# Query and key low parts moved forward, strided reciprocals, and one look-ahead low part ahead of the gated product, in an attention and FFN layer

## The reference

```
qu, ku, vu, qc, kc, vc = split(xn @ W_qkv.T)          # each 8 heads x 512 x 64
term1     = where(causal, 0, (qc*s) @ vu.T)
lookahead = where(causal, sigmoid((qu*s) @ ku.T), 0)
Su        = term1 @ lookahead.T
scores    = where(causal, -max, (qc*s) @ kc.T - silu(Su))
out       = softmax(scores) @ vc ; out @ W_out.T
```

## Time and profile before

| | |
|---|---|
| median of 3 runs | 1061.36 us (1061.29 to 1063.61) |
| profiled execution, own time | 1063.24 us |
| its span | 1061.3 us |
| TensorE busy | 1038.1 us, 98% |
| VectorE busy | 888.6 us, 84% |
| ScalarE busy | 753.2 us, 71% |
| GpSimd busy | 565.1 us, 53% |
| granted TensorE clock | full speed throughout |

### The profile page before, as it was taken

One profiled execution on the slowest core, in us unless ns is written; L12 is line 12 of the kernel. 1 busy time (PEld: TensorE's weight loads), 2 busy tenths in 40 slices (PEclk: granted clock), 3 DMA queues, 4 the chain that ended last, 5 costly groups with the idle time before them and its releaser, 6 DMA issues.

```text
span 1061.3 us, 21352 instructions
## 1 busy us (share of the span) xinstructions
PE 1038.1 (98%) x7472; PEld 926.5 (87%) x7472; DVE 888.6 (84%) x1831; ACT 753.2 (71%) x1453; POOL 565.1 (53%) x630
## 2 busy tenths in 40 slices
PE   6999999999999999999999999999999989999997
PEld 5888888888888888888888888888888878899987
DVE  5798899889988998899889988998888878767665
ACT  6678777877787778777877787778777765443433
POOL 5365565556555655565556555656555546322230
PEclk9999999999999999999999999999999999999999
DMA  5054555565555555555555555654545965566632
GB/s 198 1 110 95 137 133 120 130 146 124 116 134 135 135 110 140 123 147 110 140 113 156 110 140 103 161 110 110 122 99 114 244 197 198 168 200 221 206 121 61
DMA packets 362716, 144.30 MB, mean 136 GB/s; under 512 B 254832, under 2 KB 343664, under 8 KB 360560
## 3 DMA queue, kind: packets, MB, share of 16 engines
q1 hardware_dynamic: 362608, 142.91, 53.2%
HBM read 76.55 MB, written 66.32 MB: 135 GB/s over the span
## 4 chain that ended last, share of the span: by engine, by line
PE 64%; ACT 16%; DVE 11%; POOL 4%; issue 4%; DMA 0%; ACTq 0%; POOLq 0%; DVEq 0%
PE X L850 17%; PE X L765 13%; PE X L1001 8%; PE X L992 6%; ACT prob L1191 5%; PE X L902 4%; PE X L834 4%; PE X L818 4%; PE X L804 4%; POOL prob L685 4%; ACT L_s L1175 3%; ACT T_s L1169 3%; PE X L789 3%; DVE gate L1485 2%; ACT PT_s L1221 2%
## 5 line engine op out<-in xcount | busy, mean ns | idle before, releaser
L685 POOL TENSOR_SCALAR prob<-prob,inv 128x512 f32<-128x512 f32 (+3 forms) x256 | 304.0, 1203 | 20.4 <-DVE inv L1515 20.4
L850 PE MATMUL X<-L_s,T_s 128*128 128x128 f32 (+3 forms) x1920 | 275.9, 301 | 2.5 <-DVE L_s L1471 2.2
L850 PEld LDWEIGHTS X<-L_s,T_s 128*128 128x128 f32 x1920 | 265.4, 189 | 13.9 <-issue 3.3
L765 PE MATMUL X<-xT,W 128*128 128x512 f32 (+1 forms) x972 | 244.5, 398 | 0.0
L765 PEld LDWEIGHTS X<-xT,W 128*128 128x128 f32 x972 | 175.6, 191 | 40.7 <-issue 0.4
L1183 ACT ACTIVATE gate<-X 128x1024 f32<-128x1024 f32 (+1 forms) x96 | 84.8, 884 | 157.2 <-PE X L850 157.1
L675 POOL TENSOR_SCALAR_AFFINE_SELECT T_s<-T_s 128x512 fp32r<-128x512 f32 x128 | 106.2, 842 | 102.1 <-DVE T_s L1478 102.1
L1191 ACT ACTIVATE prob<-prob,least 128x512 f32<-128x512 f32 (+3 forms) x256 | 141.8, 587 | 1.5 <-DVE least L1503 1.5
L1478 DVE TENSOR_TENSOR T_s<-X,T_s 128x1024 fp32r<-128x1024 f32 (+1 forms) x96 | 100.5, 1047 | 43.9 <-ACT T_s L1169 43.3
L659 POOL TENSOR_SCALAR_AFFINE_SELECT gate<-gate 128x256 f32<-128x256 f32 (+1 forms) x96 | 47.2, 495 | 163.1 <-DVE gate L1485 163.1
L1503 DVE CUSTOM_DVE_ANT_0 prob<-X,gate 128x512 f32<-128x512 f32 (+3 forms) x256 | 112.5, 486 | 8.0 <-issue 6.8
(11 more groups left out here) (111 smaller groups left out, 1876.0 us busy)
## 6 DMA issues: line engine op xcount, KB each, us to landing
PT_s<-prob_raw SPq DMA_DIRECT2D x210, 128.0 KB, 2.6
heads_out<-o_s SPq DMA_DIRECT2D x62, 256.0 KB, 3.5
prob_raw<-prob SPq DMA_DIRECT2D x120, 128.0 KB, 2.7
prob_raw<-prob SPq DMA_DIRECT2D x120, 96.0 KB, 2.8
xT_copy<-xT SPq DMA_DIRECT2D x8, 1024.0 KB, 7.8
w_split<-w_parts SPq DMA_DIRECT2D x22, 256.0 KB, 2.9
W<-w_split SPq DMA_DIRECT2D x12, 384.0 KB, 5.5
xT<-xT_copy SPq DMA_DIRECT2D x4, 1024.0 KB, 6.9
```

Source lines behind the costliest of these rows:

```text
L685: last = pool.tensor_scalar(v, v, inv[:, h, w - 1:w], None, ALU.mult)
L765: last = pe.matmul(out[:, tokens], sh.W[:, a, k, cols], xT[:, c, k, tokens], start=(n == 0), stop=(n == 3 * KD - 1))
L850: last = pe.matmul(both[:, h, at:at + (J + 1) * P], T_s[:, h, a, to:to + P], L_s[:, h, c, WIDE[J + 1]:WIDE[J + 1] + (J + 1) * P], start=(J ...
```

## The change

Three edits, all on VectorE. The order of all other engines is as before.

- `inverse` did one reciprocal for each head and row (2, 4 and 2 instructions of one column for groups 0, 1 and 2). It now does one instruction for each group, over both heads and the group's rows with a step of 2.
- The low parts of the next pair's query and key (`low_proj` of QU and KU) stood after `inverse(g - 1, 2)`. The query's now stands ahead of `low_T(g, 2)`, the key's ahead of `inverse(g - 1, 1)`.
- `low_L(g, 2)` stood behind `gated_of(0, 0)` and `hidden(0, 0)`, which exist in the last step alone. It now stands ahead of them.

```diff
             def inverse(g, j):
-                for h in range(2):
-                    for i, w in enumerate(ROWS[j]):
-                        if h == 0 and i == 0:
-                            dve.wait_ge(exp_done, after(g, j))
-                        last = dve.reciprocal(inv[:, h, w - 1:w], total[:, h, w - 1:w])
-                last.then_inc(inv_done, 1)
+                rows = slice(min(ROWS[j]) - 1, max(ROWS[j]), 2)
+                dve.wait_ge(exp_done, after(g, j))
+                dve.reciprocal(inv[:, :, rows], total[:, :, rows]).then_inc(inv_done, 1)
...
                 if g == 0:
                     low_L(g, 0)
+                if ahead:
+                    low_proj(g + 1, QU, par)
                 low_T(g, 2)
                 if g > 0:
                     low_L(g, 0)
+                if ahead:
+                    low_proj(g + 1, KU, par)
                 if back1:
                     inverse(g - 1, 1)
                 low_L(g, 1)
+                low_L(g, 2)
                 if part == LAST and q == 3:
                     gated_of(0, 0)
                     hidden(0, 0)
-                low_L(g, 2)
                 if g == 0:
                     low_W(9)
                 if back1:
                     inverse(g - 1, 2)
-                if ahead:
-                    low_proj(g + 1, QU, par)
-                    low_proj(g + 1, KU, par)
                 if back1 and g - 1 < SQUARED:
                     row_in_squares(g - 1, 3)
```

## The result

The changed kernel takes **1054.04 us** (median of 4 runs, 1053.88 to 1054.62), the kernel before 1062.48 in the same session (4 runs, 1061.29 to 1064.02). The ratio is 0.9918, with a 95% interval from 0.9906 to 0.9931, so 8.4 us or 0.8% faster; the profiled spans are 1052.5 and 1061.3. The direction is as forecast.

The account below looks back on a forecast made before the run. TensorE was taken as the bound, with only its own gaps to win. Five batches 4.0, two other late boundaries 0.7 and the last step 0.56 made 5.3 us: median 1061.36 to 1056.0 us, range 1054.8 to 1059.4.

Parts of the forecast that it names:

- Five batches 4.0: Late term1 after q=0 and q=1: five whole batches lose 4.0 us, 0.8 each, against 20 steps of 26.51 us.
- (b): VectorE, reciprocals: one strided instruction replaces group 1's four, saving 0.18 us ahead of low_L 1; the other calls save 0.06 each.
- (a): VectorE: query's and key's low parts, 1.18 us, leave the stretch behind low_L for gaps of 0.51 and 0.61 us.
- (c): Behind low_L 2 everything moves 1.24 us forward; 1.17 left from second row_in_squares; term1's wait gone with 0.4 us to spare.
- a sign of being wrong: Listed signs: a new sum_up wait for low_L each step, or a VectorE gap before the second row_in_squares, waiting for GpSimd.
- all steps last 26.5 us: Sign of being right in TensorE's timeline, with term1 starting 0.69 us after the look-ahead in every step.
- (d): Last step: low_L 2 goes first, sum_up starts 1.02 us sooner, 0.56 left because the transposes need GpSimd's norm; bounds 0.4 to 1.02.
- the rival rule of the prediction: Skill's rule that two-SBUF-input VectorE and GpSimd instructions exclude each other: last-step low_L 2 about 0.9 us later, gain 0.4 or less.
- Partly given back: Rival: the boundary wait is only halved, through GpSimd's later second norm or ScalarE's gate; 1058.6 us, chance 0.12.
- no change: Rival: only the last step gains, by its lower bound, as the chain binds at GpSimd every step; 1061.0 us, chance 0.07.
- slower: Rival: low parts do not fit ahead of low_L, so low_L 2 comes too late for sum_up; 1066 us, chance 0.05.
- More: Rival: last step gives its whole 1.02 us and sooner norms take 0.3 us of unpriced waits; 1055.2 us, chance 0.06.

Follow-up runs that it names:

- the order alone: Only the query's and key's low parts moved, old reciprocals and old last step, against the kernel before: 1061.35 us, ratio 0.9976.
- eight spare reciprocals: Changed kernel plus eight one-column reciprocals into an unread tile ahead of group 1's merged one: 1085.33 us, ratio 1.0207 against the kernel before.

## Why the prediction was right in direction and too small

**The step that failed** is the first sentence of the sum: "Five batches 4.0", made against steps of "26.50 and 26.52 us" that I called undisturbed. I had taken the shortest steps for TensorE's own, because TensorE was "busy" throughout them. They held a wait for GpSimd's `norm` that the busy time hides. With that, the reciprocals were priced as cover for part (b)'s overrun and at nothing in the sum. Measured, the reciprocals of group 1 are worth 30 steps x 0.14 us: 20 steps of 26.37 instead of 26.51 are the 2.8 us by which the five batches gave more than 4.0. The kernel with only those four undone (795.53) against the changed one (789.77) gives 5.8, of which 1.4 are the two longer steps (27.29 and 27.20). The parts do not add up: the reciprocals alone gain 4.4 us, the order alone 2.4, both 8.5. Most of the missing 1.7 us are the 27.39 and 27.30 us steps of the order alone, which the sooner reciprocals bring down to 0.2 us too much.

**(a), the low parts in VectorE's gaps: right, but not free.** In the changed kernel VectorE has no gap before `low_T`, and `term1` is on time in all steps. The order alone removes what was forecast: 26.51 to 26.56 in all four places of the batch, but for the two steps in which VectorE is late and the gap that had absorbed it is full.

**(b), the strided reciprocal: right in size, wrong in worth.** It takes 0.18 us and its successor starts 0.09 us after it (555.81 and 555.90 in step g=20). `norm` starts 14.04 us after the look-ahead instead of 14.21, 0.17 sooner where 0.18 was predicted. That `low_L` 2 keeps its start was right too; that it keeps its 0.95 us was not: 0.79.

**(c), what follows `low_L` 2: right.** ScalarE's gate still releases the second `silu_of`, and VectorE waits 0.14 us ahead of the second `row_in_squares` for GpSimd (step g=21). The prediction had listed such a gap as a sign of being wrong, though its own times had the two within 0.1 us; it hides behind the slack at `term1`. The sign that did tell was the other one: "all steps last 26.5 us" did not hold.

**(d), the last step: right in kind.** `sum_up` 1.05 us sooner (1.02 predicted), bounded then by `norm` at the transposes, 0.79 (0.56 predicted). `norm` ended 0.38 us sooner after the look-ahead (20.13 to 19.75), not 0.18, since beside its sooner start it lasted 6.19 us instead of 6.41. That it lasts less comes with `low_L`'s new place: with this alone `norm` ends at 19.93, with the reciprocals alone at 19.96. Not foreseen was that ScalarE's copy would become `sum_up`'s last wait; it costs 0.1 us. `low_L` 2 (847.21 to 847.99) did not wait for the end of `norm`'s instruction beside it, at 848.11, so the rival rule of the prediction did not hold here either.

**The rivals.** "Partly given back", "no change" and "slower" did not occur. "More" had the right mechanism, unpriced waits behind sooner `norm`s, but at 0.3 us, where the 30 steps gave 3.8 more than forecast; its 1055.2 should by its own terms be 1055.3, which changes nothing. The eight spare reciprocals show what "slower" would have looked like, at GpSimd and not, as I had it, at `low_L`.

## What to carry to other kernels

A step period is TensorE's own only if the instruction behind each hand-over doesn't start right at its producer's end: check that in the best steps too, and in the waits of the weight loads, before taking them as the floor of a sum. Where everything is periodic, 0.15 us on such a hand-over counts once for every step, so a small edit that is "only overhead" can be worth as much as the reordering beside it. When two engines get in each other's way, the pause between two instructions can matter more than their length. And a gap of an engine that does not bound is not free room: here it had absorbed a delay of 0.35 us that came in a single step.

## What the runs showed of the hardware

GpSimd and VectorE slow each other, but not evenly. A GpSimd instruction that starts under a `low_L` (a VectorE instruction with two inputs in SBUF) ends 1.0 to 1.1 us after that `low_L` has ended: 2.02 us when the `low_L` ends after 0.9 us of it, 2.54 and 2.63 us when a second `low_L` follows at once. The same 128x384 instruction takes 1.24 us later in the step (step g=20 of before), so most of it is done after the `low_L`. "At once" is narrow: in those steps the second `low_L` starts 0.08 to 0.10 us before the record of the first ends, as VectorE's instructions do when they wait for nothing. Where it started 0.03 us before that end (step g=24 of the changed kernel) or 0.04 us after it (g=21 of before), GpSimd's instruction already ended 1.1 us after the first one. The opposite direction is mild. The next `low_L`, started while GpSimd's instruction still runs, lasts 0.95 us if it starts 0.04 us after the first one's end (step g=21 of before), 0.79 at 0.20 us, and 0.68 at 0.51 us: as if held off until 0.31 us after the first one's end in both of the first cases, and not until GpSimd is done. VectorE's low parts, with one input in PSUM, take 0.68 us beside a running GpSimd instruction and do not hold it up (2.02 us with one inside it).

The Trainium skill's page "SBUF — State Buffer", section "SBUF: two separate sides", says that whichever of the two starts first keeps the shared port for its whole instruction while the other is fully blocked. For GpSimd waiting on VectorE the runs are in keeping with it (2.54 us with two `low_L` ahead of its end). For VectorE behind GpSimd they don't: by that rule `low_L` 2 of step g=20 would end at 558.21 + 0.68 = 558.89, and it ended at 558.09.

Two things stay open. What holds VectorE up by 0.35 us in a single step, in the kernel before as well, no row shows: the profile has it as "issue", and it is not always the same step (g=20 before, g=24 in the changed kernel). And it was not tried why the granted clock fell after a wait of 2.20 us in one profiled execution and not in the other.
